# The scratch of the spread keys in HBM: laid out by feature and part instead of by part and feature

## What is computed

```python
h = _layernorm(x, axis=-1) * (1 + ca) + sa
qkv = h @ qkv_w.T + qkv_b
q, k, v = jnp.split(qkv, 3, axis=-1)          # 16 heads of 8 features
q, k = apply_rope(q), apply_rope(k)
attn = jnp.einsum('bqhd,bkhd->bhqk', q, k) * scale
attn = softmax(where(mask, -1e9, attn))
out = jnp.einsum('bhqk,bkhd->bqhd', attn, v)
x = x + ga * (out @ proj_w.T + proj_b)
```

## Time and profile before

| what | us |
|---|---|
| median of 3 runs | 441.01 (440.32 to 444.39) |
| the profiled execution | 443.15 |
| its span, first to last instruction | 441.4 |
| PE busy in the span | 390.9 |
| DVE busy | 329.3 |
| ACT busy | 256.8 |
| POOL busy | 126.1 |
| mean granted TensorE clock | 0.988 |

### The profile page before, as it was taken

One profiled execution on the slowest core, in us unless ns is written; L12 is line 12 of the kernel. 1 busy time (PEld: TensorE's weight loads), 2 busy tenths in 40 slices (PEclk: granted clock), 3 DMA queues, 4 the chain that ended last, 5 costly groups with the idle time before them and its releaser, 6 DMA issues.

```text
span 441.4 us, 15622 instructions
## 1 busy us (share of the span) xinstructions
PE 390.9 (89%) x6599; PEld 253.1 (57%) x6599; DVE 329.3 (75%) x730; ACT 256.8 (58%) x447; POOL 126.1 (29%) x163
## 2 busy tenths in 40 slices
PE   2778899888999989998899999998998889988885
PEld 2327555555656755666457654765566646753653
DVE  6659995886886988878986997699866777541176
ACT  8203465565676756765666665766665457566523
POOL 6714310430343043503342234304330220040020
PEclk9989999999999999999999999999999899998999
DMA  7056363243314233242415251323233050011001
GB/s 214 22 161 169 99 218 88 70 116 102 104 45 119 75 101 93 80 122 49 137 50 139 64 138 48 117 72 99 67 113 86 16 146 6 25 45 27 3 1 49
DMA packets 26050, 38.53 MB, mean 87 GB/s; under 512 B 5796, under 2 KB 20716, under 8 KB 23692
## 3 DMA queue, kind: packets, MB, share of 16 engines
q1 hardware_dynamic: 25980, 37.53, 29.8%
HBM read 26.35 MB, written 8.65 MB: 79 GB/s over the span
## 4 chain that ended last, share of the span: by engine, by line
PE 41%; DMA 18%; DVE 13%; ACT 10%; POOL 6%; issue 5%; SPq 5%; ACTq 0%; POOLq 0%; DVEq 0%
PE o_bank L611 10%; DMA kf<-k_scr 9%; PE d_bank L528 7%; DVE negmax L978 6%; PE t_bank L593 6%; PE s_bank L548 5%; DMA rden<-r_scr 4%; ACT probs L827 4%; PE a_bank L528 3%; DMA r_scr<-rden_c 2%; POOL parts L1303 2%; PE s_bank L528 2%; SPq L440 2%; PE t_bank L528 2%; POOL o_n L1325 2%
## 5 line engine op out<-in xcount | busy, mean ns | idle before, releaser
L978 DVE TENSOR_REDUCE negmax<-s_bank 128x1 f32<-128x512 f32 (+7 forms) x368 | 192.9, 566 | 56.9 <-PE s_bank L554 54.6
L827 ACT ACTIVATE probs<-t_bank 128x512 f32<-128x512 f32 x288 | 163.0, 594 | 89.8 <-PE t_bank L598 84.5
L548 PE MATMUL s_bank<-kf,qf 126*64 126x512 bf16 (+7 forms) x1024 | 118.7, 293 | 11.8 <-DMA kf<-k_scr 6.2
L593 PE MATMUL t_bank<-qf,kf 128*64 128x512 bf16 (+7 forms) x1024 | 113.3, 290 | 10.8 <-ACT probs L827 9.8
L611 PE MATMUL o_bank<-probs,v 128*32 128x512 f32 (+7 forms) x1024 | 75.1, 412 | 0.0
L548 PEld LDWEIGHTS s_bank<-kf,qf 126*64 126x64 bf16 x1024 | 50.6, 111 | 40.6 <-DVE negmax L978 19.9
L554 PE MATMUL s_bank<-causal,identb 128*64 128x64 bf16 x1024 | 72.6, 195 | 0.0
L598 PE MATMUL t_bank<-causal_t,identb 128*64 128x64 bf16 x1024 | 64.8, 195 | 0.0
L593 PEld LDWEIGHTS t_bank<-qf,kf 128*64 128x64 bf16 x1024 | 41.4, 110 | 35.1 <-ACT probs L827 14.4
L598 PEld LDWEIGHTS t_bank<-causal_t,identb 128*64 128x64 bf16 x1024 | 48.1, 111 | 9.3 <-issue 0.2
L554 PEld LDWEIGHTS s_bank<-causal,identb 128*64 128x64 bf16 x1024 | 47.1, 112 | 8.3 <-issue 8.1
(11 more groups left out here) (145 smaller groups left out, 455.9 us busy)
## 6 DMA issues: line engine op xcount, KB each, us to landing
qf<-q_scr SPq DMA_DIRECT2D x15, 576.0 KB
kf<-k_scr SPq DMA_DIRECT2D x45, 192.0 KB
q_scr<-parts SPq DMA_DIRECT2D x24, 128.0 KB, 1.7
k_scr<-parts SPq DMA_DIRECT2D x24, 128.0 KB, 1.7
xa<-in_x SPq DMA_DIRECT2D x8, 256.0 KB, 3.9
o_t<-o_raw SPq DMA_DIRECT2D x60, 32.0 KB, 2.4
rden<-r_scr SPq DMA_DIRECT2D x15, 128.0 KB
out_y<-count SPq DMA_DIRECT2D x7, 256.0 KB, 6.7
```

Of the source, the lines that this page charges most:

```text
L548: nc.tensor.matmul(bank[C * a:C * (a + 1), col:col + keys], qf[0:KS, slot, 2 * p + a, C * i:C * (i + 1)], kf[0:KS, slot, 2 * p + a, 0:keys ...
L593: nc.tensor.matmul(bank[C * a:C * (a + 1), col:col + w], kf[0:KX, slot, 2 * p + a, C * kb:C * (kb + 1)], qf[0:KX, slot, 2 * p + a, C * kb: ...
L827: nc.scalar.activation(probs[:, v, :], t_bank[u % 2][:, :], ACT.Exp, scale=SCALE).then_inc(e_done, 1)
L978: last = nc.vector.tensor_reduce(own[:, i, p:p + len(same)], cols, AX.X, ALU.max, negate=True)
```

## The change

The scratch tensors get their dimensions in another order, and loads and stores are written for it. `k_scr` is now (slot, feature, part, head, position): the 24 key rows of a batch stand in the order in which `kf` has them, 16 KB apart, and of each a half takes a run of 8 KB. A load of keys so reads 24 rows of 4096 elements with one step. A store of a key part, which wrote one block of 128 KB, now writes 8 blocks of 16 KB that stand 48 KB apart. For `q_scr` the order in memory stays what it was; heads and positions are only written as one run.

```diff
-    q_scr = nc.dram_tensor("q_scr", (2, NPART, P, SEQ), BF16, kind="Internal").ap()
-    k_scr = nc.dram_tensor("k_scr", (2, NPART, P, SEQ), BF16, kind="Internal").ap()
+
+    q_scr = nc.dram_tensor("q_scr", (2, NPART, HD, H, SEQ), BF16, kind="Internal").ap()
+    k_scr = nc.dram_tensor("k_scr", (2, HD, NPART, H, SEQ), BF16, kind="Internal").ap()
...
-                scr, stored_parts = ((q_scr, q_stored), (k_scr, k_stored))[qk]
-                sp.dma_start(scr[b % 2, j], parts[:, qk, j, :]).then_inc(stored_parts, 16)
+                to, stored_parts = ((q_scr[b % 2, j], q_stored), (k_scr[b % 2, :, j], k_stored))[qk]
+                sp.dma_start(to, parts[:, qk, j, :]).then_inc(stored_parts, 16)
...
-                q_rows = q_scr[b % 2].rearrange("i (d h) c -> (i d) h c", h=H)[:, heads]
-                sp.dma_start(qf[0:FR, n % RING, own],
-                             q_rows.unsqueeze(1).to_broadcast([NPART * HD, NPART, many, SEQ])).then_inc(done, 16)
+                q_rows = q_scr[b % 2].rearrange("i d h c -> (i d) (h c)")[:, run]
+                sp.dma_start(qf[0:FR, n % RING, own].rearrange("r h c -> r (h c)"),
+                             q_rows.unsqueeze(1).to_broadcast([NPART * HD, NPART, run.stop - run.start]))\
+                    .then_inc(done, 16)
...
-                k_rows = k_scr[b % 2].rearrange("j (d h) c -> d j h c", h=H)[:, :, heads]
+                k_rows = k_scr[b % 2].rearrange("d j h c -> (d j) (h c)")[:, run]
                 m = HD * NPART
                 for i in range(NPART):
-                    sp.dma_start(kf[m * i:m * (i + 1), n % RING, own], k_rows).then_inc(done, 16)
+                    sp.dma_start(kf[m * i:m * (i + 1), n % RING, own].rearrange("r h c -> r (h c)"), k_rows)\
+                        .then_inc(done, 16)
```

More of the change, by code:

```diff
@@ L394, in store_part @@
                 reach(sp, feat[(2 * b - 3) % RING], 16 * FEAT_DMAS * ((2 * b - 3) // RING + 1))
-                scr, stored_parts = ((q_scr, q_stored), (k_scr, k_stored))[qk]
-                sp.dma_start(scr[b % 2, j], parts[:, qk, j, :]).then_inc(stored_parts, 16)
+                to, stored_parts = ((q_scr[b % 2, j], q_stored), (k_scr[b % 2, :, j], k_stored))[qk]
+                sp.dma_start(to, parts[:, qk, j, :]).then_inc(stored_parts, 16)
             def spread_queries(n, own=slice(0, HH), done=None):
                 b, half = divmod(n, 2)
-                heads = slice(HH * half + own.start, HH * half + own.stop)
-                many = own.stop - own.start
+                run = slice(SEQ * (HH * half + own.start), SEQ * (HH * half + own.stop))
                 done = done or feat[n % RING]
```

## The result

The changed kernel takes 448.08 us (median of 20 runs, 444.20 to 452.05); the kernel before, timed beside it, 441.2 us (20 runs, 435.74 to 445.67). The ratio is 1.0169, with a 95% interval of 1.013 to 1.0207: the change makes the kernel slower by 1.7%, some 7 us. I had forecast 437.3 us, in a range of 434.9 to 442.6. The measured time lies outside it, on the other side.

What follows compares the result with a forecast made beforehand. PE, busy 390.9 of 441.4 us, was taken as the bound, waiting 6.2 us for keys; 4.74 us recovered, about 1 returning as other waits, left 3.7: from the median 441.01 to 437.3 us, range 434.9 to 442.6.

Steps and rivals of the forecast that it cites:

- What bounds the kernel, and where a spread counts: PE is the engine to keep fed; a transfer counts only where PE waits: 6.2 us for key loads, six places.
- No longer runs: Loads already moved in 8 KB runs (2,358 packets), so no gain can come from packet size.
- Twelve engines for the loads, eight for the store: Key loads go from eight DMA engines to twelve, the key store from sixteen to eight.
- The key loads' rate: Key loads moving alone rise from a mean of 135 to 175 GB/s, landing 0.70 to 1.63 us earlier.
- The 4.74 us of recovered stalls: Sum of PE's stalls for keys recovered in six halves, each the smaller of stall and earlier landing.
- Issues on SP: On SP a key load's issue falls from 0.65 to 0.40 us; a key store's rises from 0.325 to 0.59.
- The key store: In even halves the store comes up to 0.77 us later; the query load hides all but 0.27.
- Nothing: Rival: 24 destination partitions set the keys' rate, landings stay, three even halves pay 0.27 us each: 441.8 us, chance 0.29.
- Slower: Rival: key store's 0.77 us unhidden and loads no faster, six even halves lose 4.6 us: 445.6 us, chance 0.08.
- my last sign of being wrong: The prediction is wrong if PE's waits for kf grow in the even halves; no size given.
- The condition I had set for it: In even halves, the slower case decides once the key store's delay outgrows the gain of the loads.

Runs made afterwards that it cites:

- wide8: Kernel before, but each key load writes every third of 72 partitions instead of 24 neighbours, still on eight engines: 436.78 us against 439.62, ratio 0.9941.
- store8: Kernel before with only the key store changed, to 8 blocks 48 KB apart on eight engines: 442.76 us against 439.62, ratio 1.0041.
- load12: Kernel before with only the key loads changed, to 24 rows with one step on twelve engines: 441.98 us against 439.62, ratio 1.0056.
- wide_right: Kernel before with key loads into every third partition, each row named three times, products right, eight-engine store moved to queries: 435.99 us against 439.80, ratio 0.9934.

## Why the prediction was wrong

- **What bounds the kernel, and where a spread counts: right.** The stalls for kf are the machine's: wide8 took 5.1 of their 6.2 us away and gained 0.59%, 2.6 us of 439.6 (by the interval 0.8 to 4.4). By the middle value half of what the stalls gave back was lost elsewhere, 2.5 us where I had put 1.
- **No longer runs: right,** 2,358 packets before and after.
- **Twelve engines for the loads, eight for the store: right** by the loads' shares of 0.74 to 0.80, and by the store's 1.0 us of traffic at no more than six tenths.
- **The key loads' rate: the step that failed.** I took 175 GB/s, "since twelve engines now write into 24 partitions where a query load writes into 72", as a middle between 135 and 211. It stayed at 111 to 155 (mean 124 of the five stretches, 135 before). Those words already held the reason for the lower end: eight against twelve engines and 24 against 72 partitions changed together in the earlier trace rows, and I averaged two theories instead of choosing. wide8 parts them: 167 to 200 GB/s on eight engines. The 4.74 us of recovered stalls rested on this term, and it is zero: PE's wait for kf didn't fall by 4.7 us but rose by 4.7, from 6.2 to 10.9.
- **Issues on SP: right,** 0.36 us (0.40) for the loads and 0.63 us (0.59) for the stores. The shorter issues bought nothing, since the loads behind them are bound elsewhere.
- **The key store: somewhat too small, and its cover wrong.** 1.0 us of traffic instead of 0.5 was right, and so was 0.3 us more of issue, but the landing came 1.0 us later (1.67 to 2.67 us) and not 0.77; the remaining 0.2 us stay unexplained. I let the query load in front hide all but 0.27. At n = 14 0.56 us of it reached the last key load's landing, and in the whole change new stalls stand in n = 6 and n = 10. Alone the late store costs 0.4% (store8, nothing to 0.8).
- **The rivals.** "Nothing" had the right rate and the wrong sum: it counted 0.8 us for the store where the change lost 7. "Slower", in its own place, the even halves, with 4.6 us, came nearest and had a chance of 0.08. Both its parts came true, and so did my last sign of being wrong, growing waits for kf in the even halves. But it left out the growth in the odd half n = 3, left out that the loads on twelve engines cost something themselves (load12, 0.6%), and left out that the two together seem to cost more than their sum. The condition I had set for it, that the store's delay outgrows the gain of the loads, is met at once when that gain is zero: "nothing" and "slower" shared the same rate and differed only in what the query load hides. I gave this rate 0.37 in all, and 0.63 to loads that get faster.

The Trainium skill's rule, "SBUF — State Buffer", section "Door 1: The DMA port swizzle (why [64,N] ≈ [32,N])", is borne out as an upper bound: 24 neighbouring partitions reach six of its ports, an estimate of 163 GB/s, and no stretch of narrow key loads alone goes above 161 (load12). I had cited it for a rival and not let it set the rate: my 175 lay above its bound. It doesn't give the 111 to 155 themselves. My reading of it for 72 partitions was wrong too: by its table they reach ten ports, an estimate of 272 GB/s, and not eight or nine, so the 161 to 210 of the wide loads and the 221 of a query load are held by something that no run here shows.

## What to carry to other kernels

When a load is slow, ask which end is narrow before giving it more DMA engines: look at the DMA share together with the GB/s, and compare with another load that differs in one thing only. If share and width of the destination change together, try the width by itself; here a stride of three partitions in the destination was one line, worth 0.6%, and the twelve engines gained nothing that could be measured. A layout that is neater for the reader of a scratch tensor may make its writer's DMA weaker (here sixteen engines to eight, 0.5 to 1.0 us), and that counts where a load waits for the store.

## What was not expected of the hardware

- Eight DMA engines moved 8 KB rows from HBM at 167 to 200 GB/s, up to 25 GB/s each, little less than twelve (193 to 210), when the rows landed in every third partition of 72. Into 24 neighbouring partitions eight moved 118 to 152 (before and store8) and twelve 111 to 161 (after and load12).
- A source whose every row is named three times in one DMA of eight rows (wide_right) moved about as fast as one of 24 different rows: 161 to 202 GB/s against 167 to 200 (wide8).
- More engines on a load that is bound at its destination seem to do harm: 1.0056 (1.0015 to 1.0098) for the loads alone. By what way isn't shown.
